# The x rows of a gated state-space block added by TensorE and copied out by ScalarE, and four products by C moved from GpSimd to VectorE

## The chip, the cores and the metric
One core of one Trainium2 chip runs the whole kernel. The metric is the device time of one execution in microseconds (us).

## The reference, cut to what matters
```
# ctx (4,512,256), x (4,512,512)
u  = silu(conv(ctx @ in_w.T) + b)                  # (4, 512 channels, 512 times)
dt, B, C from u @ xp_w.T ; dt = softplus(dt @ dt_w + bias)
state = state * exp(dt * A) + (dt * u) * B         # scan over time, 16 states per channel
y = sum over states(state * C) + D * u
y = y * silu(layernorm(x))                         # the gate
x = x + tanh(g_xattn) * y
x = x + tanh(g_ffn) * ffn(layernorm(x))            # w3(silu(w1 x) * (w2 x)), quantized
```

## The kernel before, in words
The state-space part is cut into 128 steps k. A step holds 128 channels (a block q), two of the 16 states and all 512 times, or, in the last two of the four batches (SPLIT), four states and half the times. Its tile hh (six buffers, NH = 6) is 128 x 1024. Eight steps make one group g = k // 8, whose y is summed in one PSUM bank, bank_y. The written-out order of each engine goes by a loop over slots k:

- GpSimd (POOL): product of step k by C, times_c, L808 and L813, then the product of step k+4 by B, times_b, L697 and L703. The latter waits until step k-2 has been summed out of its buffer (LEAD = 4, NH = 6). Small GpSimd operations (rh_pool, L1108) stand between them.
- VectorE (DVE): the scan of step k+3 (L765, L768), and for steps in BY_VECTOR also its product by C (times_c_vector, L791). Such a scan writes into the PSUM bank da that holds the exponentials, and the exponentials of step k+2, which use the same bank, wait for the product.
- ScalarE (ACT): the exponentials of step k+4 (exp, L731 and L738, into one of two PSUM banks da), which wait for the scan of step k+2, and keep_state (L751), which saves the last state of a first half.
- TensorE (PE): sums(k-1), eight transposes into bank_y (L846). At the first step of a group it waits for bank_y to be free and puts D*u into it first (L834, the seed).

The second part (the gated MLP, on tiles of 128 rows, TILE gives the slot of each) runs in the same loops: a_tensor and b_tensor (L1001, L1010), tanh_scalar (L1022), gated_vector (L1029, L1035), square_scalar (L1040), hq_scalar (L1104), transposes ht_tensor (L1155) and their copies hqt_scalar (L1166), out_tensor (L1186). At slots 49, 64, 87 and 99 dt_scalar (L337, L340) computes softplus, with a table load before it and one after it, for the next groups. z_scalar (L518, L519) and xt_tensor (L968) prepare gates and MLP inputs.

At slots 40, 48, ..., 120 the group g = k // 8 - 1 is finished. In gate, VectorE multiplies bank_y by the gate (L571) and adds the rows of x, writing x2 (L586, or L580 in the SPLIT batches). The mark ("y", g) of that add is what sums(k) of TensorE waits for. Groups 0 to 3 go another way (y_keep and y_first), and group 15 stands in the tail after the loops. In slots 38 to 79 sums(k-1) is TensorE's first work of a slot; the copy hqt_scalar(i, 1) is late in ScalarE's slot.

Of the kernel before, what the change touches and what calls it, by code (L numbers as in the profile page):

```python
# [12 lines left out]
P = 128  # L13
# [3 lines left out]
NE = DM // P  # L17
# [40 lines left out]

BY_VECTOR = (14, 16, 25, 45, 49, 53, 62, 67, 68, 73, 77)


def c_by_vector(k):
# [27 lines left out]
def build(nc, book, x, ctx_t, in_w, xp_w, dt_w, weights, consts, out):  # L92
    u_dram = nc.dram_tensor("u_scratch", [NB, P, NE, L], F32).ap()
    xd_dram = nc.dram_tensor("xd_scratch", [NB, ROWS, L], F32).ap()
    with ExitStack() as ctx:
# [114 lines left out]
        BV, BP = line("first_products"), line("first_rows_of_b")  # L210
        ZV, ZA, ZG, ZP = line("z_vector"), line("z_scalar"), line("z_pool"), line("z_tensor")
        WV, WA, WP = line("weight_vector"), line("weight_scalar"), line("weight_tensor")
        YV, YA = line("y_vector"), line("y_scalar")
        MV, MA, MP, MG = line("mlp_vector"), line("mlp_scalar"), line("mlp_tensor"), line("mlp_pool")

        hl = sb("hl", [P, NE, NS])
# [348 lines left out]
            YV.did(v.tensor_tensor(columns(x2[0], g), by_rows(bank_t[:, :]), columns(xin, g), ALU.add), ("p", g))  # L565

        def gate(v, g):
            b, q = g // NE, g % NE
            v.wait_ge(s_sum, STEPS * (g + 1))
            v.wait_ge(*ZA.of(("gT", g)))  # L570
            YV.did(v.tensor_tensor(bank_y[:, :], bank_y[:, :], gbuf[:, q, :], ALU.mult))  # L571
            if b in SPLIT:
                h, p = q // 2, q % 2
                if p == 0:
                    for t in (2 * h, 2 * h + 1):
                        v.wait_ge(*d_out[t].of(NE * (b - 2) + t))
                v.wait_ge(*YV.now())
                to, rows = [of[:, 2 * h:2 * h + 2, 2 * p * P:2 * (p + 1) * P].rearrange("p c (j d) -> p j c d", j=2)
                            for of in (x2[b % 2], xin)]
                YV.did(v.tensor_tensor(to, bank_y[:, :].rearrange("p (j c d) -> p j c d", j=2, c=2), rows, ALU.add),  # L580
                       ("y", g))
                return
            if g == NE:
                v.wait_ge(*WA.of(("sign", NW - 1)))
            v.wait_ge(*YV.now())
            YV.did(v.tensor_tensor(columns(x2[b % 2], q), by_rows(bank_y[:, :]), columns(xin, q), ALU.add), ("y", g))  # L586

        def x_done(i):

            b = i // NE  # L590
            if b == 0:
                return YV.of(("p", NE - 1))
            return YV.of(("y", NE * b + (1 if b in SPLIT and i % NE < 2 else NE - 1)))

# [222 lines left out]
        def sums(pe, k):  # L817
            b, q, s = where(k)
            g = k // STEPS
            if s == 0:  # L820
                if g > NE:
                    pe.wait_ge(*YV.of(("y", g - 1)))
                elif g:
                    pe.wait_ge(*YA.of(("y", g - 1)))
                else:
                    pe.wait_ge(*PV.of("diag_d"))
                    pe.wait_ge(*BV.of(1))
                if g < NE:
# [375 lines left out]
        with nc.Block() as block:  # L1204
# [214 lines left out]
            def _(act):  # L1419
# [62 lines left out]
                for k in range(38, 80):  # L1482
                    for i in range(END):
                        c = k - tile_slot(i) - 1
                        if 0 <= c < NCH:
                            tanh_scalar(act, i, c)
                    if k + LEAD - 2 < ALL:
                        keep_state(act, k + LEAD - 2)
                    for i in range(END - 1):
                        if k == tile_slot(i) + 9:  # L1490
                            hqt_scalar(act, i, 2)
                    if k + LEAD < ALL:
                        exp(act, k + LEAD)
                    for i in range(END - 1):
                        if k == tile_slot(i) + 8:
                            hqt_scalar(act, i, 0)
                    for first, n, done in TURNS:
                        if k == done + 3:
                            center_scalar(act, first, n)
                    for i in range(END + 1):  # L1500
                        if k == tile_slot(i) - 2:
                            xr_scalar(act, i)
                    for n in PAIR:
                        if k == PAIR[n]:
                            dt_scalar(act, 2 * n)
                            dt_scalar(act, 2 * n + 1)
                    for i in range(END):
                        if k == tile_slot(i) + 7:
                            hq_scalar(act, i, 0)
                            hq_scalar(act, i, 1)  # L1510
                    for i in range(END - 1):
                        if k == tile_slot(i) + 9:
                            hqt_scalar(act, i, 3)
                    for i in range(END):
                        if k == tile_slot(i) + 2 or k == tile_slot(i) + 4:
                            square_scalar(act, i, k - tile_slot(i) - 1)
                    for b in range(NB):
                        if k == (13, 34, 66, 94)[b]:
                            z_scales(act, b)
                    for i in range(END - 1):  # L1520
                        if k == tile_slot(i) + 8:
                            hqt_scalar(act, i, 1)
                    for i in TILES:
                        if i >= NE and k == z_turn_slot(i):
                            z_turn_scalar(act, i)
                    for i in TILES:
                        if k == z_slot(i):
                            z_scalar(act, i)
                    for i in range(END + 1):
                        if k == tile_slot(i) - 1:  # L1530
                            xqt_scalar(act, i)
                    for first, n, done in TURNS:
                        if k == done + 5:
                            rows_scalar(act, first, min(n, END - first))
                            if first + n > END:
                                rows_scalar(act, END, 1)
                for k in range(80, SLOTS):
                    for first, n, done in TURNS:
                        if k == done + 3:
                            center_scalar(act, first, n)  # L1540
                    for i in range(END):
                        c = k - tile_slot(i) - 1
                        if 0 <= c < NCH:
                            tanh_scalar(act, i, c)
                    if k + LEAD < ALL:
                        exp(act, k + LEAD)
                    if k + LEAD - 2 < ALL:
                        keep_state(act, k + LEAD - 2)
                    for i in range(END + 1):
                        if k == tile_slot(i) - 2:  # L1550
# [38 lines left out]
                    for i in range(END - 1):  # L1589
                        if k == tile_slot(i) + 8:  # L1590
                            hqt_scalar(act, i, 1)
                act.preload_act_table_set("silu_and_others")
                tanh_scalar(act, 13, 0)
                hq_scalar(act, 12, 0)
# [42 lines left out]
            def _(pe):  # L1637
# [39 lines left out]
                for k in range(38, 80):  # L1677
# [34 lines left out]
                    for i in range(END + 1):  # L1712
                        c = k - tile_slot(i)
                        if 0 <= c < NCH:
                            b_tensor(pe, i, c)
                for k in range(80, SLOTS):
                    if 0 <= k - 1 < ALL:
                        sums(pe, k - 1)
# [32 lines left out]
                    for i in range(END + 1):  # L1751
                        c = k - tile_slot(i)
                        if 0 <= c < NCH:
                            b_tensor(pe, i, c)
                sums(pe, 125)
                sums(pe, 124)
                ab_tensor(pe, 13, 1)
# [282 lines left out]
```

## Time and profile before

| | |
|---|---|
| Device time, median of 3 runs | 658.8 us (657.06, 658.80, 659.78) |
| Profiled execution, span from first to last instruction | 658.2 us (its own device time is not listed apart) |
| GpSimd (POOL) busy | 588.0 us, 89% |
| VectorE (DVE) busy | 585.5 us, 89% |
| ScalarE (ACT) busy | 535.6 us, 81% |
| TensorE (PE) busy | 503.0 us, 76% |
| Mean granted TensorE clock | 0.919 |

Busy times are sums over the whole span. Times in the rows below are counted from the start of the span. A time in square brackets behind an instruction is how long its engine stood idle before it, and which instruction ended that.

### The profile page before, as it was taken

What the parts mean: (1) busy time and instruction counts of PE and PEld (TensorE: products, weight loads), DVE (VectorE), ACT (ScalarE), POOL (GpSimd) and SP (SyncE); (2) the same over time, 40 slices, a digit from 0 to 9 for tenths busy, and PEclk for the clock granted to TensorE, in tenths of its full rate; (3) what the DMA queues carried; (4) which work ended last, traced back from release to release, by engine and by line L of the source; (5) the groups of instructions that cost most, each with busy time, mean ns of one, the idle gap of its engine ahead of it and who ended that gap; (6) DMA issues with size and microseconds to landing.
All of it is one profiled execution on the core that took longest, in us unless ns stands there. A gap on an engine that the chain in (4) does not pass through costs nothing.

```text
span 658.2 us, 7987 instructions
## 1 busy us (share of the span) xinstructions
PE 503.0 (76%) x2560; PEld 310.1 (47%) x2560; DVE 585.5 (89%) x771; ACT 535.6 (81%) x997; POOL 588.0 (89%) x289
## 2 busy tenths in 40 slices
PE   8798888993565777788658586877767786768997
PEld 3254534552453445555535354554444544446554
DVE  6779779998998899999889999999897999999765
ACT  6754757788999688978888798898899898897764
POOL 1399999998999999999999999999999999999331
PEclk9898989998766979999796999889899999899999
DMA  5698687579950100256500000046700000000001
GB/s 184 199 406 295 209 298 277 192 274 392 394 223 6 33 0 1 75 171 234 179 21 1 32 1 16 1 146 224 269 17 0 17 1 16 1 17 17 0 18 47
DMA packets 24473, 80.77 MB, mean 123 GB/s; under 512 B 2464, under 2 KB 5152, under 8 KB 21360
## 3 DMA queue, kind: packets, MB, share of 16 engines
q1 hardware_dynamic: 24432, 80.27, 33.7%
q8 instruction: 20, 0.33, 0.2%
q14 instruction: 21, 0.17, 0.1%
HBM read 72.53 MB, written 7.73 MB: 122 GB/s over the span
## 4 chain that ended last, share of the span: by engine, by line
POOL 31%; DVE 23%; PE 15%; ACT 15%; issue 10%; DMA 5%; SPq 2%; DVEq 0%; POOLq 0%; ACTq 0%
POOL hh L703 9%; DVE hh L768 9%; POOL hh L813 8%; POOL hh L808 7%; POOL hh L697 6%; ACT da L731 4%; DVE hh L765 3%; DMA wq<-x 3%; DVE room L1029 2%; PE da L1186 2%; PE bank_y L846 2%; PE bank_b L1010 2%; DVE sm L1074 2%; PE bank_a L1001 1%; ACT room L1166 1%
## 5 line engine op out<-in xcount | busy, mean ns | idle before, releaser
L768 DVE TENSOR_TENSOR_SCAN hh<-da,hh 128x1024 f32<-128x1024 f32 x85 | 193.4, 2280 | 3.4 <-ACT da L738 2.3
L846 PE MATMUL bank_y<-ident,hh 128*128 128x128 f32 x1024 | 144.5, 291 | 9.0 <-POOL hh L813 8.7
L846 PEld LDWEIGHTS bank_y<-ident,hh 128*128 128x128 f32 x1024 | 129.6, 152 | 37.4 <-issue 16.1
L808 POOL TENSOR_TENSOR hh<-hh,cc 128x1024 f32<-128x1024 f32 x60 | 141.7, 2364 | 1.7 <-ACT hl L751 1.5
L813 POOL TENSOR_TENSOR hh<-hh,cc 128x1024 f32<-128x1024 f32 x57 | 134.7, 2363 | 0.0
L703 POOL TENSOR_TENSOR hh<-pair,bb 128x1024 f32<-128x1024 f32 x30 | 70.7, 2358 | 26.3 <-DMA bb<-xd_scratch 23.9
L765 DVE TENSOR_TENSOR_SCAN hh<-da,hl,hh 128x256 f32<-128x256 f32 x128 | 85.4, 730 | 0.0
L703 POOL TENSOR_TENSOR hh<-wq,bb 128x1024 f32<-128x1024 f32 x32 | 75.5, 2367 | 2.4 <-PE bank_y L846 2.4
L697 POOL TENSOR_TENSOR hh<-wq,bb 128x1024 f32<-128x1024 f32 x32 | 75.8, 2370 | 0.8 <-PE bank_y L846 0.8
L697 POOL TENSOR_TENSOR hh<-pair,bb 128x1024 f32<-128x1024 f32 x32 | 75.2, 2352 | 1.2 <-PE bank_y L846 1.2
L738 ACT ACTIVATE da<-pair,cst 128x511 f32<-128x511 f32 x64 | 41.3, 679 | 23.5 <-DVE hh L768 23.5
L731 ACT ACTIVATE da<-wq,cst 128x256 f32<-128x256 f32 x128 | 53.3, 464 | 7.8 <-DVE hh L765 7.5
L731 ACT ACTIVATE da<-pair,cst 128x255 f32<-128x255 f32 x128 | 53.0, 461 | 1.7 <-DVE hh L768 1.7
L1001 PE MATMUL bank_a<-wq,room 128*128 128x512 fp8e4 x120 | 33.6, 405 | 26.5 <-DVE room L1029 23.9
L738 ACT ACTIVATE da<-wq,cst 128x511 f32<-128x511 f32 x64 | 41.4, 683 | 8.9 <-DVE hh L768 8.7
L1022 ACT ACTIVATE room<-bank_a,sm 128x512 f32<-128x512 f32 x58 | 39.2, 676 | 7.9 <-PE bank_a L1001 7.6
L1186 PE MATMUL bank_t<-wq,room 128*128 128x512 fp8e4 x192 | 43.4, 379 | 2.1 <-ACT room L1166 2.1
L1001 PE MATMUL bank_a<-wq,xqT 128*128 128x512 fp8e4 x112 | 32.4, 417 | 16.0 <-DVE room L1029 16.0
L1166 ACT ACTIVATE room<-bank_t,sm 128x512 bf16<-128x512 f32 x53 | 35.8, 676 | 10.8 <-PE bank_t L1155 10.7
L1029 DVE SCALAR_TENSOR_TENSOR room<-room,bank_a 128x512 f32<-128x512 f32 x52 | 35.3, 679 | 9.3 <-ACT room L1022 8.9
L1010 PE MATMUL bank_b<-wq,room 128*128 128x512 fp8e4 x120 | 33.4, 404 | 0.0
L968 PE MATMUL bank_t<-ident,room 128*128 128x128 f32 x56 | 10.2, 312 | 27.0 <-ACT room L951 15.2
(269 smaller groups left out, 1085.7 us busy)
## 6 DMA issues: line engine op xcount, KB each, us to landing
bb<-xd_scratch SPq DMA_DIRECT2D x32, 512.0 KB, 5.1
cc<-xd_scratch SPq DMA_DIRECT2D x32, 512.0 KB, 7.5
wq<-weights SPq DMA_DIRECT2D x12, 1024.0 KB, 6.7
stage<-weights SPq DMA_DIRECT2D x8, 1024.0 KB, 5.6
xin<-x SPq DMA_DIRECT2D x4, 1024.0 KB, 5.5
room<-weights SPq DMA_DIRECT2D x4, 1024.0 KB, 8.0
u_scratch<-wq SPq DMA_DIRECT2D x6, 512.0 KB, 3.0
wq<-x SPq DMA_DIRECT2D x2, 1024.0 KB, 18.2
```

Of the source, the lines that this page charges most:

```text
L697: ins = g_.tensor_tensor(quarters(flat(hh[k % NH])), du2[g % 4][:, HALF * (q % 2):HALF * (q % 2 + 1)].unsqueeze(1).to_broadcast([P, 4, HAL ...
L703: ins = g_.tensor_tensor(hh[k % NH][:, :, :], du2[g % 4].unsqueeze(1).to_broadcast([P, GN, L]), bb[:, s * GN:(s + 1) * GN, :], ALU.mult)
L731: ins = act.activation(da[:, j, first:HALF], dt2[g % 4][:, HALF * (q % 2) + first:HALF * (q % 2 + 1)], ACT.Exp, scale=a_neg[:, q, n + j:n ...
L738: ins = act.activation(dbank[k % 2][:, j, 1:L], dt2[g % 4][:, 1:L], ACT.Exp, scale=a_neg[:, q, s * GN + j:s * GN + j + 1])
L765: ins = v.tensor_tensor_scan(to[:, t], da[:, t], h[:, t], hl[:, q, n + j:n + j + 1], ALU.mult, ALU.add)
L768: ins = v.tensor_tensor_scan(to, da, h, 0.0, ALU.mult, ALU.add)
L808: ins = g_.tensor_tensor(quarters(flat(hh[k % NH])), quarters(flat(hh[k % NH])), cc[:, n:n + 4, t], ALU.mult)
L813: ins = g_.tensor_tensor(hh[k % NH][:, :, :], hh[k % NH][:, :, :], cc[:, s * GN:(s + 1) * GN, :], ALU.mult)
L846: mm = pe.matmul(bank_y[:, (first + c) * P:(first + c + 1) * P], flat(hh[k % NH])[:, at:at + P], ident[:, :], start=False, stop=(s == STEP ...
L1001: mm = pe.matmul(a[:, :], xqT[i % 2][:, k, :], w1q[:, k, c * 512:(c + 1) * 512], start=(k == 0), stop=(k == NE - 1))
L1029: MV.did(v.scalar_tensor_tensor(out=th[c % 2], in0=th[c % 2], scalar=1.0, in1=a[:, :], op0=ALU.add, op1=ALU.mult), ("g", i, c))
L1186: mm = pe.matmul(bank_g(i)[:, :], hqT[:, f, :], w3q[:, f, :], start=(f == 0), stop=(f == KF - 1))
```

## The change
The rows of x are no longer added by VectorE for groups 4 to 14. TensorE adds them in bank_y, by a float32 matmul with the identity, and ScalarE copies bank_y into x2. TensorE's step stands last in its slot k (k = 40, 48, ..., 120), and so does ScalarE's copy in its own slot; sums(k), at the head of TensorE's next slot, waits for the copy. Group 15 keeps both steps on VectorE. Steps 58, 65, 100 and 107 are added to BY_VECTOR, so their product by C goes from GpSimd to VectorE. From slot 80 on, keep_state of a step in BY_VECTOR goes ahead of the exponentials in ScalarE's slot. Readers of x2 wait for ScalarE's mark.

```diff
-BY_VECTOR = (14, 16, 25, 45, 49, 53, 62, 67, 68, 73, 77)
+BY_VECTOR = (14, 16, 25, 45, 49, 53, 58, 62, 65, 67, 68, 73, 77, 100, 107)
...
         def gate(v, g):
-            b, q = g // NE, g % NE
+            q = g % NE
             v.wait_ge(s_sum, STEPS * (g + 1))
             v.wait_ge(*ZA.of(("gT", g)))
-            YV.did(v.tensor_tensor(bank_y[:, :], bank_y[:, :], gbuf[:, q, :], ALU.mult))
...
+            YV.did(v.tensor_tensor(bank_y[:, :], bank_y[:, :], gbuf[:, q, :], ALU.mult), ("gated", g))
+            if g == NB * NE - 1:
...
+        def x_add_tensor(pe, g):
+            pe.wait_ge(*YV.of(("gated", g)))
+            if g % NE == 0:
+                pe.wait_ge(*d_x.of(g // NE))
+            if g // NE in SPLIT:
+                for j in range(2):
+                    mm = pe.matmul(bank_y[:, 2 * P * j:2 * P * (j + 1)], ident[:, :], y_place(xin, g)[:, j, :, :],
+                                   start=False, stop=(j == 1), skip_group_check=True)
+            else:
+                mm = pe.matmul(bank_y[:, :], ident[:, :], y_place(xin, g), start=False, stop=True,
+                               skip_group_check=True)
+            YP.did(mm, ("x", g))
+
+        def y_scalar(act, g):
+            b, q = g // NE, g % NE
+            act.wait_ge(*YP.of(("x", g)))
...
+            YA.did(act.activation(y_place(x2[b % 2], g), rows, ACT.Copy), ("y", g))
...
             if s == 0:
-                if g > NE:
-                    pe.wait_ge(*YV.of(("y", g - 1)))
-                elif g:
+                if g:
                     pe.wait_ge(*YA.of(("y", g - 1)))
...
+                    if k % STEPS == 0 and PER < k < ALL:
+                        y_scalar(act, k // STEPS - 1)
...
+                    if c_by_vector(k + LEAD - 2):
+                        keep_state(act, k + LEAD - 2)
                     if k + LEAD < ALL:
                         exp(act, k + LEAD)
-                    if k + LEAD - 2 < ALL:
+                    if k + LEAD - 2 < ALL and not c_by_vector(k + LEAD - 2):
                         keep_state(act, k + LEAD - 2)
...
+                    if k % STEPS == 0 and PER < k < ALL:
+                        x_add_tensor(pe, k // STEPS - 1)
```

## Rows read from the trace of the kernel before

**Rows 1.** The page: busy time, share and instructions of each engine.
```profile
PE 503.0 (76%) x2560; PEld 310.1 (47%) x2560; DVE 585.5 (89%) x771; ACT 535.6 (81%) x997; POOL 588.0 (89%) x289
```

**Rows 2.** Five of 837 pieces of the last-ending chain: start, length, what.
```profile
241.62 0.52 POOL sm L1108
...
325.66 1.28 ACT L337
...
482.99 1.16 ACT room L1040 x2
...
518.50 2.36 POOL hh L697
...
607.08 4.65 POOL hh L808 x2
```

**Rows 3.** Busy time in stretches: length; PE, PEld, DVE, ACT, POOL; clock, DMA share, GB/s.
```profile
264.00:319.00 55.00, 42.29 (x266) 27.99 (x264) 54.07 (x57) 45.80 (x80) 55.00 (x26) 1.00 0.47 162
...
518.00:612.00 94.00, 69.81 (x434) 45.89 (x433) 89.29 (x147) 80.05 (x166) 93.44 (x46) 0.98 0.03 12
```

**Rows 4.** Instruction groups by line and shape: busy us, mean ns, idle before.
```profile
L808 POOL TENSOR_TENSOR hh<-hh,cc 128x1024 f32<-128x1024 f32 x60 | 141.7, 2364 | 1.7 <-ACT hl L751 1.5
...
L791 DVE TENSOR_TENSOR hh<-da,cc 128x1024 f32<-128x1024 f32 x11 | 13.5, 1225 | 0.4
...
L545 ACT ACTIVATE gbuf<-bank_t,sm 128x512 f32<-128x512 f32 x12 | 8.0, 668 | 0.0
...
L251 PE MATMUL bank_a<-wq,room 128*128 128x512 f32 x16 | 7.7, 602 | 0.0
```

**Rows 5.** VectorE in order of time: a gate (slot 40) and a product by C.
```profile
222.36 0.69 DVE L571 TENSOR_TENSOR bank_y<-bank_y,gbuf 128x512 f32<-128x512 f32 x1
223.16 0.69 DVE L586 TENSOR_TENSOR stage<-bank_y,xin 128x512 f32<-128x512 f32 x1
223.77 2.28 DVE L768 TENSOR_TENSOR_SCAN hh<-da,hh 128x1024 f32<-128x1024 f32 x1
...
234.22 1.22 DVE L791 TENSOR_TENSOR hh<-da,cc 128x1024 f32<-128x1024 f32 x1
235.36 1.21 DVE L1074 TENSOR_REDUCE sm<-room 128x1 f32<-128x1024 f32 x1
```

**Rows 6.** Slots 48 and 49 in order of time.
```profile
260.13 0.76 ACT L519 ACTIVATE bank_a<-xin,sm 128x512 f32<-128x512 f32 x1
...
262.73 0.63 PE L968 MATMUL bank_t<-ident,room 128*128 128x128 f32 x4 [1.62 <-DVE room L1193]
...
264.42 0.60 ACT L337 ACTIVATE pair<-bank_a 128x512 f32<-128x512 f32 x1 [0.97 <-PE bank_a L300]
```

**Rows 7.** Slots 63 to 65 in order of time.
```profile
320.14 0.22 DVE L1093 TENSOR_SCALAR sm<-sm 128x1 f32<-128x1 f32 x1 [1.15 <-POOL sm L1108]
...
320.82 2.37 ACT L1104 ACTIVATE wq<-wq,sm 128x1024 f32<-128x1024 f32 x2
...
327.68 1.04 PE L846 MATMUL bank_y<-ident,hh 128*128 128x128 f32 x8
...
328.96 0.68 ACT L1166 ACTIVATE room<-bank_t,sm 128x512 bf16<-128x512 f32 x1
...
329.79 0.63 PE L1155 MATMUL bank_t<-ident,wq 128*128 128x128 f32 x4 [1.07 <-ACT room L1166]
...
334.27 2.29 DVE L768 TENSOR_TENSOR_SCAN hh<-da,hh 128x1024 f32<-128x1024 f32 x1 [1.04 <-ACT da L731]
```

**Rows 8.** ScalarE in slot 89, in order of time.
```profile
440.12 1.27 ACT L731 ACTIVATE da<-wq,cst 128x256 f32<-128x256 f32 x3 [0.20 <-DVE hh L765]
```

**Rows 9.** Slot 104 in order of time: ScalarE's last gate operation, TensorE's seed, GpSimd's wait.
```profile
519.07 0.55 ACT L519 ACTIVATE bank_a<-xin,sm 128x256 f32<-128x256 f32 x1
...
516.50 1.05 PE L834 MATMUL bank_y<-diag_d,pair 128*128 128x128 f32 x8
...
518.50 2.36 POOL L697 TENSOR_TENSOR hh<-pair,bb 128x1024 f32<-128x1024 f32 x1 [0.44 <-PE bank_y L846]
```

More of the change, by code:

```diff
@@ L212, in build @@
         WV, WA, WP = line("weight_vector"), line("weight_scalar"), line("weight_tensor")
-        YV, YA = line("y_vector"), line("y_scalar")
+        YV, YA, YP = line("y_vector"), line("y_scalar"), line("y_tensor")
         MV, MA, MP, MG = line("mlp_vector"), line("mlp_scalar"), line("mlp_tensor"), line("mlp_pool")
@@ L567, in gate, with y_place @@
         def gate(v, g):
-            b, q = g // NE, g % NE
+            q = g % NE
             v.wait_ge(s_sum, STEPS * (g + 1))
             v.wait_ge(*ZA.of(("gT", g)))
-            YV.did(v.tensor_tensor(bank_y[:, :], bank_y[:, :], gbuf[:, q, :], ALU.mult))
+            if g == NE:
+                v.wait_ge(*WA.of(("sign", NW - 1)))
+            YV.did(v.tensor_tensor(bank_y[:, :], bank_y[:, :], gbuf[:, q, :], ALU.mult), ("gated", g))
+            if g == NB * NE - 1:
+                for t in (2, 3):
+                    v.wait_ge(*d_out[t].of(NE + t))
+                v.wait_ge(*YV.now())
+                YV.did(v.tensor_tensor(y_place(x2[1], g), bank_y[:, :].rearrange("p (j c d) -> p j c d", j=2, c=2),
+                                       y_place(xin, g), ALU.add), ("y", g))
+        def y_place(of, g):
+            b, q = g // NE, g % NE
+            if b in SPLIT:
+                h, p = q // 2, q % 2
+                return of[:, 2 * h:2 * h + 2, 2 * p * P:2 * (p + 1) * P].rearrange("p c (j d) -> p j c d", j=2)
+            return columns(of, q)
+        def x_add_tensor(pe, g):
[11 more added lines that the diff above has]
+        def y_scalar(act, g):
+            b, q = g // NE, g % NE
+            act.wait_ge(*YP.of(("x", g)))
             if b in SPLIT:
@@ L575, in gate @@
                     for t in (2 * h, 2 * h + 1):
[L576 to L586, printed above, removed]
+                        act.wait_ge(*d_out[t].of(NE * (b - 2) + t))
+                rows = bank_y[:, :].rearrange("p (j c d) -> p j c d", j=2, c=2)
+            else:
+                rows = by_rows(bank_y[:, :])
+            YA.did(act.activation(y_place(x2[b % 2], g), rows, ACT.Copy), ("y", g))
         def x_done(i):
@@ L592, in x_done @@
                 return YV.of(("p", NE - 1))
-            return YV.of(("y", NE * b + (1 if b in SPLIT and i % NE < 2 else NE - 1)))
+            g = NE * b + (1 if b in SPLIT and i % NE < 2 else NE - 1)
+            return (YV if g == NB * NE - 1 else YA).of(("y", g))
         def sum_slot(i):
@@ L1591, in _ @@
                             hqt_scalar(act, i, 1)
+                    if k % STEPS == 0 and PER < k < ALL:
+                        y_scalar(act, k // STEPS - 1)
                 act.preload_act_table_set("silu_and_others")
@@ L1715, in _ @@
                             b_tensor(pe, i, c)
+                    if k % STEPS == 0 and PER < k < ALL:
+                        x_add_tensor(pe, k // STEPS - 1)
                 for k in range(80, SLOTS):
@@ L1754, in _ @@
                             b_tensor(pe, i, c)
+                    if k % STEPS == 0 and PER < k < ALL:
+                        x_add_tensor(pe, k // STEPS - 1)
                 sums(pe, 125)
```

## The prediction, made before the changed kernel was run
> **What bounds the kernel now.** I read the page's busy shares first, then the chain that ended last, then the busy time by stretches, and last the order of time around each slot that the change touches. The page says that no engine is the bound by itself: GpSimd and VectorE are both at 89% [rows 1]. The stretches sharpen that: from 264 to 319 us GpSimd is busy 55.00 of 55 us and VectorE 54.07; from 518 to 612 us they have 93.44 and 89.29 of 94 [rows 3]. So a busy share can't say which of the two a saved microsecond is saved on. The chain can. It goes along GpSimd up to its small operation at 241.62, then leaves it, and until 518.50 runs through VectorE, ScalarE and TensorE, among others through ScalarE's softplus stage at 325.66; from GpSimd's product at 518.50 it stays on GpSimd to the last products at 607.08 [rows 2]. What I take from it: between 242 and 518 us, GpSimd's work hides behind a VectorE and ScalarE path that is just as long; after 518 us VectorE's work hides behind GpSimd's. I therefore follow the change along this path and add up what each edit does to it. A plus is lateness.
>
> **The parts and their prices.**
>
> *Add of x taken off VectorE, 11 times.* At slot 40 the gate starts at 222.36, the add at 223.16 and the scan at 223.77 [rows 5]. Without the add the scan could start some 0.6 us behind the gate, as the scan does behind the add: 1.41 - 0.61 = 0.8 us saved on VectorE's path. Eleven times that is 8.8 us, but only where VectorE's path is the one that counts. At slot 40 GpSimd's is, so that one is worth nothing.
>
> *Product by C on VectorE, 4 times.* It takes 1225 ns against 2364 ns on GpSimd [rows 4]. The next instruction starts 1.14 us behind it, 0.1 before its end (235.36 against 234.22 + 1.22) [rows 5]. The product needs its scan's result and can't overlap that scan's end in this way, so I add 0.1 and the wait itself: 1.3 us more for VectorE in all. GpSimd is relieved of 2.4 us each time.
>
> *TensorE's matmul with the identity.* A float32 matmul 128 x 512 by two records of 602 ns, pipelined, is between 0.6 and 1.2 us [rows 4]; I take 0.9. It is hidden where TensorE would wait for ScalarE's copy anyway, which is so at slots 48, 64 and 104 (below).
>
> *ScalarE's copy.* By the 128 x 512 copies out of PSUM, 668 ns, some 0.6 from start to start [rows 4]; 11 of them, 7 us more on ScalarE.
>
> *The new wait.* This is what decides. sums(k), at the head of TensorE's slot k+1, used to wait for VectorE's add. Now it waits for a copy that is the last thing in ScalarE's slot k. Behind sums(k) on TensorE stand the transposes and MLP matmuls of slot k+1, and behind sums(k) by its buffer stands GpSimd's product by B of step k+6. On ScalarE the next tanh and exponentials stand behind the copy. Slot by slot:
>
> - Slot 48: ScalarE ends its z work at 260.13 + 0.75 = 260.9 [rows 6]. Copy to 261.5, seed and sums about 0.9 us each [rows 7, 9] to 263.3; the transpose L968 behind them starts then instead of at 262.73, where it had waited 1.62 us for VectorE. The softplus stage waits for TensorE (0.97 us before L337) [rows 6], so the path gets +0.6, and VectorE's saving of this slot is lost.
> - Slot 56: VectorE's path counts: -0.8. Its product of step 58 stands just ahead: +1.3.
> - Step 65: VectorE has 1.15 us idle in which the product would nearly fit, but the exponentials of step 67 wait for it, and behind these ScalarE is solid (L1104 at 320.82 for 2.37, then the exponentials of step 68) [rows 7]: +1.3 on ScalarE's path. Sum so far +2.4.
> - Slot 64: the softplus stage. Before, sums(64) was done at 328.7, and the transpose L1155 waited for ScalarE's L1166 (328.96 to 329.64) until 329.79 [rows 7]. ScalarE's copy comes only behind that L1166: 329.6 to 330.2; then seed and sums 1.8 us, then L1155 at 332.1. That is 2.3 us later, and ScalarE's next copy, the table load and exponentials behind it, and the scan at 334.27, which waited 1.04 us for them [rows 7], all follow. +2.3. Sum +4.7.
> - Slots 72 and 80: -0.8 and -0.7; ScalarE has room there. Sum +3.2.
> - Slot 88: ScalarE had 0.20 us idle before the exponentials at 440.12 [rows 8]. A copy of 0.67 ahead of them makes it 0.5 late, and the hq and tanh behind them hand that to VectorE: +0.5 instead of -0.8. Sum +3.7.
> - Slot 96: tanh one copy later, so -0.3 only; then the product of step 100 ahead of the work that ScalarE's 482.99 waits for [rows 2]: +1.3. Sum +4.7.
> - Slot 104: ScalarE ends z at 519.62 [rows 9], 0.8 earlier with the add gone. Copy to 519.45, seed to 520.5, sums to 521.4, where it was 516.50 + 0.9 + 1.04 = 518.4 [rows 9]: +3.0. GpSimd's product at 518.50 already waited 0.44 us for these sums. Sum +7.7.
> - From there GpSimd sets the end, without the product of step 107: -2.4 [rows 4]. Slots 112 and 120 shorten only VectorE, which by then has 4.7 - 3 x 0.8 + 1.3 = +3.6 and hides again. Sum +5.3.
>
> 0.6 - 0.8 + 1.3 + 1.3 + 2.3 - 0.8 - 0.7 + 0.5 - 0.3 + 1.3 + 3.0 - 2.4 = +5.3 us. The products of 58, 65 and 100 give nothing: they relieve GpSimd of 7.1 us where it is off the path, and what it gains it waits for at sums(104). xin is loaded later too, by the SP queue, which waits for ScalarE's mark; some 6 us later at slot 65 (the mark goes from some 324 to 330 us), hidden since the first z work on it is in slot 68, three slots of two GpSimd products each, some 14 us, later [rows 4].
>
> The profiled execution spans 658.2 us; the median of the runs is 658.8, 0.6 above it, so the same sum on the median is **664.1 us**.
>
> **Bounds of what the trace doesn't show.** The matmul of x with its two ends (0.6, 1.2) is off the path in the three slots that cost most; at 1.2 it adds 0.3 at up to three others, +1. A copy is 0.57 to 0.7. The three stalls (0.6, 2.3, 3.0) come from queue orders; each is bounded below by nothing (work before it absorbs it) and above by adding ScalarE's own lateness again, some 0.7. So the likeliest case has its own range of +2.5 to +9, 661.3 to 668.
>
> **A rule against this.** The Trainium skill (Perfetto Trace Analysis, Identifying the Most-Contended Engine) says to take the engine with the highest occupancy as the one to optimize first, and that occupancy is a fair measure for VectorE, ScalarE and GpSimd. By this rule the sum would be the first rival's.
>
> **The rivals.**
>
> 1. *GpSimd alone bounds.* Four products less, 4 x 2.364 = 9.5 us [rows 4], come off the end: 649.3. For it: 55.00 of 55 us [rows 3]. Against it: the chain leaves GpSimd for 276 us [rows 2], and VectorE stands at 54.07 of 55. Chance 0.10. This ends on the other side, and decides if VectorE and ScalarE can move up by as much as GpSimd.
> 2. *VectorE alone bounds and the new waits cost nothing.* -11 x 0.8 + 4 x 1.3 = -3.6 us: 655.2. For it: it is the engine most on the chain from 264 to 319, idle 0.93 of 55 us. Against it: the 0.20 us and the 1.07 us above show that ScalarE and TensorE have no room in slots 64 and 88. It decides if the copy is done by the time the add used to be. Chance 0.12.
> 3. *One of the two large stalls is absorbed* (2.3 at slot 64 or 3.0 at slot 104), for instance because sums(104) is late but GpSimd has caught up before: +2.3 to +3, 661.1 to 661.8, no change that can be told. Chance 0.22.
> 4. *The copy costs more*: ScalarE waits for TensorE at the end of every slot and hands it on each time, 0.7 us at six more slots: +9.5, 668.3. For it: ScalarE is 80.05 of 94 us busy at the end [rows 3], but with gaps of a microsecond before most exponentials, so I hold it unlikely. Chance 0.11.
>
> My forecast has 0.45. A measurement of this kernel tells about 0.5% from no change, here 3.3 us. Faster by more (under 655.5): all of rival 1 and most of 2, 0.20. Within: the rest of 2, rival 3, 0.24. Slower by more (over 662.1): forecast and rival 4, 0.56. The range goes from rival 2 to rival 4, 655 to 669, and leaves out rival 1 and the edges.
>
> **What the changed profile would show.** If right: the chain still leaves GpSimd before slot 48 and passes, near 330 us, through the ScalarE copy into x2, then L834, L846 and L1155; L1155 stands 2 us and more behind L1166; the scan of step 69 has an idle time of some 4 us instead of 1.04, ended by ScalarE; GpSimd's product of step 110 waits some 3 us or more for bank_y. GpSimd is busy near 579 us, VectorE near 583, ScalarE near 543. Rival 1 or 2 is right if the copies stand well ahead of the seeds, and these start as soon behind the gates as before. The weakest points are slot 104, since a late sums(104) counts only as far as nothing else has held GpSimd up, and the claim that GpSimd's relief before slot 104 is worth nothing.

## The result and the profile after

The changed kernel takes **666.2 us** (median of 6 runs, 665.3 to 667.7) where the kernel before, on the same chip in the same minutes, takes 659.1 (6 runs, 657.1 to 662.0). The ratio is **1.0108, 95% interval [1.0087, 1.0129]**: 7.1 us slower, between 5.7 and 8.5. The forecast was 664.1, slower, with 655 to 669 as the range. The profiled execution spans 663.6 us, 5.4 more than that of before; the medians lie 7.1 apart, so the profiled executions show some 1.7 us less of a difference than the medians do. Single runs of the kernel before lie up to 2.8 us from its median, and I compare places within one pair of traces to some tenths only where the start of the stretch agrees. The trace of the changed kernel runs 0.3 us ahead of that of before up to slot 40, so a place that is said to be 5.2 us later has lost 5.5.

The page's first part, against [rows 1]:
```profile
PE 514.8 (78%) x2596; PEld 317.1 (48%) x2596; DVE 582.8 (88%) x764; ACT 541.9 (82%) x1012; POOL 579.3 (87%) x285
```
GpSimd has 8.7 us less work and VectorE 2.7 less; ScalarE has 6.3 more and TensorE 11.8 more. Forecast were 579, 583 and 543 for the first three. Both engines that seemed full became lighter and the kernel became slower, so what was taken away was waited for. The waits of GpSimd say at which hand-over, first of before, then of after (engine, line and what it waited for: us in total, times, longest):
```profile
POOL hh L697 <- PE bank_y L846: 2.1, 3, 0.8
```
```profile
POOL hh L726 <- PE bank_y L873: 13.8, 5, 5.9
```
GpSimd's product by B (L697, now L726) waits for the sums (L846, now L873) 11.7 us more than before. That is more than the 8.7 us it was relieved of. The copy's own line shows who waits for it, over the whole span (us, times):
```profile
L614 ACT ACTIVATE stage<-bank_y x7: 574/597/607, 224.3 to 597.4; 128x512 f32<-128x512 f32 x7
L614 ACT ACTIVATE room<-bank_y x4: 577/588/597, 366.5 to 478.4; 128x512 f32<-128x512 f32 x4
...
who waited for it (us, times):
...
  PE bank_y L861: 11.5, 11
```
The seed (L861, once L834) stands behind ScalarE's copy all 11 times, and TensorE is idle 11.5 us there.

Two stretches of the windows, against [rows 3], and between them the one that lost most (length; PE, PEld, DVE, ACT, POOL; clock, DMA share, GB/s):
```profile
264.00:319.00 55.00, 43.60 (x272) 28.81 (x271) 52.99 (x57) 46.39 (x82) 54.09 (x26) 1.00 0.48 155
319.00:346.00 27.00, 18.34 (x91) 12.75 (x90) 20.24 (x25) 22.19 (x53) 17.09 (x9) 0.75 0.22 79
...
518.00:612.00 94.00, 74.54 (x439) 48.30 (x438) 88.76 (x140) 82.99 (x176) 91.45 (x44) 0.95 0.03 12
```
From 319 to 346 us, around slot 64, GpSimd is busy 17.09 of 27 us, where it had been 26.20 before. None of the other stretches read has such a hole. In it GpSimd waits 9.9 us for the sums. Not all of that is loss: in e3 below, where the stall of slot 64 is undone, it still waits 5.9 us there, and in e9, where only the products of steps 58 and 65 have left it, 6.3 us: relieved of these it is ahead, and waits.

**Slot 64**, against [rows 7], in order of time, ScalarE first, then TensorE, VectorE and GpSimd:
```profile
326.88 0.67 ACT L1193 ACTIVATE room<-bank_t,sm 128x512 bf16<-128x512 f32 x1
...
330.87 0.68 ACT L1193 ACTIVATE room<-bank_t,sm 128x512 bf16<-128x512 f32 x1
331.43 0.61 ACT L614 ACTIVATE stage<-bank_y 128x512 f32<-128x512 f32 x1
...
329.39 1.02 PE L598 MATMUL bank_y<-xin,ident 128*128 128x512 f32 x2
332.09 1.16 PE L861 MATMUL bank_y<-diag_d,pair 128*128 128x128 f32 x8 [1.68 <-ACT stage L614]
333.09 1.04 PE L873 MATMUL bank_y<-ident,hh 128*128 128x128 f32 x8
333.96 0.60 PE L1182 MATMUL bank_t<-ident,wq 128*128 128x128 f32 x4
...
338.42 2.29 DVE L797 TENSOR_TENSOR_SCAN hh<-da,hh 128x1024 f32<-128x1024 f32 x1 [3.28 <-ACT da L760]
...
334.21 2.36 POOL L726 TENSOR_TENSOR hh<-pair,bb 128x1024 f32<-128x1024 f32 x1 [3.58 <-PE bank_y L873]
```
The reader is to see the queue: the copy L614 is the last of ScalarE's slot, behind the softplus stage and L1193; the matmul of x (L598) had been done a microsecond earlier and TensorE waits 1.68 us for the copy. The transpose L1182, which stood at 329.79 before, starts at 333.96, and the scan of step 69 at 338.42 instead of 334.27. Part of these 4.2 us was carried in: the copy starts at 331.43, 1.8 us later than the 329.6 that the prediction worked out without the lateness summed up to there.

**Slot 104**, against [rows 9]:
```profile
522.91 0.55 ACT L519 ACTIVATE bank_a<-xin,sm 128x256 f32<-128x256 f32 x1
523.40 0.57 ACT L614 ACTIVATE stage<-bank_y 128x512 f32<-128x512 f32 x1
...
521.17 1.03 PE L595 MATMUL bank_y<-xin,ident 128*128 128x256 f32 x4
524.03 1.16 PE L861 MATMUL bank_y<-diag_d,pair 128*128 128x128 f32 x8 [1.83 <-ACT stage L614]
525.02 1.04 PE L873 MATMUL bank_y<-ident,hh 128*128 128x128 f32 x8
...
526.14 2.36 POOL L726 TENSOR_TENSOR hh<-pair,bb 128x1024 f32<-128x1024 f32 x1 [2.55 <-PE bank_y L873]
```
The seed, 516.50 before, stands at 524.03. GpSimd's product stands at 526.14 instead of 518.50: +7.6 us, where the sum had +7.7.

**The chain that ended last** (start, length, what) at slot 64, and at the end, where it had been GpSimd's in [rows 2]:
```profile
330.95 0.60 ACT room L1193
331.55 0.50 ACT stage L614
...
332.09 1.16 PE bank_y L861 x8
333.25 0.89 PE bank_y L873 x8
...
334.21 2.36 POOL hh L726
```
```profile
524.49 1.14 DVE hh L820
525.65 0.18 ACT hl L780
...
526.10 1.59 ACT da L760 x4
...
597.40 0.61 ACT stage L614
...
609.12 2.58 DVE hh L794 x4
```
The first piece is the one forecast. The second is not: from slot 104 to 612 us the chain of after runs through VectorE, ScalarE and TensorE, not along GpSimd, and it enters this stretch through the product of step 107 on VectorE (L820). Later it passes through ScalarE's copy once more (L614 at 597.40, slot 120), a place where the forecast had no wait.

### The profile page after: what moved, and what is told of

Same layout as the page of the kernel before. It is cut to its first block, busy times and chain, and to the rows that moved or that the text cites. A ratio compares the mean times of both kernels' runs of the same rounds, so it can differ in the third digit from the quotient of the medians.

```text
span 663.6 us, 8066 instructions
## 1 busy us (share of the span) xinstructions
PE 514.8 (78%) x2596; PEld 317.1 (48%) x2596; DVE 582.8 (88%) x764; ACT 541.9 (82%) x1012; POOL 579.3 (87%) x285
## 4 chain that ended last, share of the span: by engine, by line
POOL 28%; DVE 22%; ACT 19%; PE 15%; issue 10%; DMA 5%; SPq 2%; POOLq 0%; DVEq 0%; ACTq 0%
POOL hh L732 9%; POOL hh L842 8%; POOL hh L726 6%; DVE hh L797 5%; DVE hh L794 5%; ACT da L760 5%; POOL hh L837 4%; DMA wq<-x 3%; DVE da L797 2%; DVE room L1056 2%; PE da L1213 2%; PE bank_b L1037 2%; PE bank_a L1028 2%; PE bank_y L873 2%; DVE sm L1101 2%
## 5 line engine op out<-in xcount | busy, mean ns | idle before, releaser
L797 DVE TENSOR_TENSOR_SCAN hh<-da,hh 128x1024 f32<-128x1024 f32 x81 | 184.2, 2279 | 5.4 <-ACT da L760 3.3
L873 PE MATMUL bank_y<-ident,hh 128*128 128x128 f32 x1024 | 145.8, 292 | 9.7 <-POOL hh L842 8.2
L873 PEld LDWEIGHTS bank_y<-ident,hh 128*128 128x128 f32 x1024 | 130.2, 152 | 39.9 <-issue 16.4
L837 POOL TENSOR_TENSOR hh<-hh,cc 128x1024 f32<-128x1024 f32 x57 | 135.1, 2370 | 2.3 <-ACT hl L780 2.2
L842 POOL TENSOR_TENSOR hh<-hh,cc 128x1024 f32<-128x1024 f32 x56 | 132.4, 2365 | 0.0
L726 POOL TENSOR_TENSOR hh<-pair,bb 128x1024 f32<-128x1024 f32 x32 | 75.5, 2366 | 13.8 <-PE bank_y L873 13.8
L726 POOL TENSOR_TENSOR hh<-wq,bb 128x1024 f32<-128x1024 f32 x32 | 76.0, 2375 | 0.0
L760 ACT ACTIVATE da<-wq,cst 128x256 f32<-128x256 f32 x128 | 53.3, 466 | 3.9 <-DVE hh L794 3.7
L760 ACT ACTIVATE da<-pair,cst 128x255 f32<-128x255 f32 x128 | 53.0, 461 | 0.8 <-DVE hh L797 0.7
L1028 PE MATMUL bank_a<-wq,room 128*128 128x512 fp8e4 x120 | 33.5, 405 | 19.8 <-DVE room L1056 17.6
L1213 PE MATMUL bank_t<-wq,room 128*128 128x512 fp8e4 x192 | 45.1, 390 | 2.0 <-ACT room L1193 2.0
L1193 ACT ACTIVATE room<-bank_t,sm 128x512 bf16<-128x512 f32 x53 | 35.9, 677 | 12.1 <-PE bank_t L1182 12.0
L1028 PE MATMUL bank_a<-wq,xqT 128*128 128x512 fp8e4 x112 | 30.7, 399 | 10.9 <-DVE room L1056 10.9
L797 DVE TENSOR_TENSOR_SCAN da<-da,hh 128x1024 f32<-128x1024 f32 x15 | 34.3, 2288 | 0.0
L1037 PE MATMUL bank_b<-wq,room 128*128 128x512 fp8e4 x120 | 33.5, 404 | 0.0
```

What stands on the lines that cost most here:

```text
L726: ins = g_.tensor_tensor(quarters(flat(hh[k % NH])), du2[g % 4][:, HALF * (q % 2):HALF * (q % 2 + 1)].unsqueeze(1).to_broadcast([P, 4, HAL ...
L760: ins = act.activation(da[:, j, first:HALF], dt2[g % 4][:, HALF * (q % 2) + first:HALF * (q % 2 + 1)], ACT.Exp, scale=a_neg[:, q, n + j:n ...
L797: ins = v.tensor_tensor_scan(to, da, h, 0.0, ALU.mult, ALU.add)
L837: ins = g_.tensor_tensor(quarters(flat(hh[k % NH])), quarters(flat(hh[k % NH])), cc[:, n:n + 4, t], ALU.mult)
L842: ins = g_.tensor_tensor(hh[k % NH][:, :, :], hh[k % NH][:, :, :], cc[:, s * GN:(s + 1) * GN, :], ALU.mult)
L1028: mm = pe.matmul(a[:, :], xqT[i % 2][:, k, :], w1q[:, k, c * 512:(c + 1) * 512], start=(k == 0), stop=(k == NE - 1))
```

## The experiments

Twelve kernels. Each ratio is to the kernel before on the same chip; us are the ratio less 1, times 659. An interval is some 1.1 to 2 us wide to either side, so two of these kernels are told apart only when they differ by some 2 us.

| kernel | ratio, 95% interval | us |
|---|---|---|
| e1 the four products only | 1.0094 [1.0068, 1.0121] | +6.2 |
| e2 the eleven adds only | 1.0109 [1.0085, 1.0133] | +7.2 |
| e3 changed, slot 64's add back | 1.0059 [1.0037, 1.0080] | +3.9 |
| e6 product 107 only | 1.0041 [1.0022, 1.0061] | +2.7 |
| e4 changed, copies of 64 and 104 early | 1.0066 [1.0048, 1.0085] | +4.3 |
| e5 changed, slot 104's add back | 1.0109 [1.0086, 1.0131] | +7.2 |
| e7 adds of 56, 72, 80, 112, 120 only | 1.0002 [0.9986, 1.0017] | +0.1 |
| e10 before, four products left out | 1.0004 [0.9986, 1.0022] | +0.3 |
| e9 products 58 and 65 only | 1.0038 [1.0017, 1.0060] | +2.5 |
| e11 four products, 100 and 107 near their scans | 1.0080 [1.0051, 1.0108] | +5.3 |
| e12 before, eleven adds left out | 0.9974 [0.9953, 0.9995] | -1.7 |
| e13 before, both left out | 0.9906 [0.9876, 0.9936] | -6.2 |

**One part alone: e1, e2, e6.**
```
e1   gate() and its users as before;  BY_VECTOR = (..., 58, ..., 65, ..., 100, 107)
e2   gate() changed;                  BY_VECTOR = (14, 16, 25, 45, 49, 53, 62, 67, 68, 73, 77)
e6   gate() as before;                BY_VECTOR = (14, ..., 77, 107)
```
e1 and e6 keep the state ahead of the exponentials, as the changed kernel does; no step from 80 on is in e2's BY_VECTOR, so nothing changes there.

> Only the four products by C (steps 58, 65, 100, 107) go to VectorE; all adds of x stay on VectorE as before. Path theory: +1.3 us for each of steps 58, 65 and 100 on the VectorE and ScalarE path up to GpSimd's product of step 110, which gives GpSimd's end 3.9 - 2.4 = +1.5; VectorE's own end, which was only 0.2 us ahead of GpSimd's, gets four times 1.3 = +5.2. So the kernel is slower by some 5 us (4 to 6), ratio 1.006 to 1.009, with the scans late behind the steps 58, 65, 100, 107. GpSimd-bound rival: faster by up to 9.5 us, ratio 0.986.

> Only the eleven adds of x move to TensorE and ScalarE; the products by C stay as before. Path theory: nothing up to slot 64 (what VectorE saves is taken by its wait for GpSimd's L1108 in slot 63, and 0.6 is lost at slot 48), +2.3 at slot 64, -1.5 at slots 72 and 80, about 0 at slots 88 and 96, +3.0 at slot 104, GpSimd solid from there: +3 to +4.5 us, ratio 1.005 to 1.007. Rival (the adds are a gain for VectorE, the busiest on the path): -3 to -8 us, ratio below 0.996.

> The kernel before with the product of step 107 alone on VectorE. In this stretch (after GpSimd's product of step 110) GpSimd is on the chain and without an idle time, so the GpSimd-bound view expects -2.4 us, ratio 0.9964. Path theory: VectorE's end was only 0.2 us ahead of GpSimd's and gets +1.3, so +1 us, ratio 1.0015, no gain from relieving the engine that the chain names.

Each part alone costs nearly as much as the whole, and e6 costs 2.7 us where the prediction's term for it was -2.4. All three cost more than was expected of them (4 to 6, 3 to 4.5 and 1 us). The trace of e6 shows the reason on VectorE, then on ScalarE (here L829 is the product by C, L806 the scan, L789 the state's copy, L769 the exponentials):
```profile
517.51 1.21 DVE L829 TENSOR_TENSOR hh<-da,cc 128x1024 f32<-128x1024 f32 x1
518.64 2.28 DVE L806 TENSOR_TENSOR_SCAN hh<-da,hh 128x1024 f32<-128x1024 f32 x1
```
```profile
518.76 0.17 ACT L789 ACTIVATE hl<-da 128x4 f32<-128x4 f32 x1 [2.20 <-DVE hh L829]
...
519.14 1.65 ACT L769 ACTIVATE da<-pair,cst 128x255 f32<-128x255 f32 x4
```
From slot 80 on the product stands last in VectorE's slot, behind a reduction, the output's operation and z. ScalarE, which must keep the state and refill the buffer that the product reads, is idle 2.20 us. GpSimd is relieved of 2.4 us, but VectorE's scans are 2.3 us later by step 111 than they were at step 107, more than the product's own 1.3. And GpSimd has to wait for that path: it is idle 2.16 us before its product by C at 523.23, until ScalarE, behind these exponentials, has kept a state (L789), and 0.81 us more before the next product by B.

In e2's trace TensorE's clock fell in slot 96 (TensorE, ScalarE, VectorE):
```profile
474.20 1.91 PE L1037 MATMUL bank_b<-wq,room 128*128 128x512 fp8e4 x4
...
475.91 1.82 PE L595 MATMUL bank_y<-xin,ident 128*128 128x256 f32 x4
...
477.76 0.60 ACT L614 ACTIVATE room<-bank_y 128x512 f32<-128x512 f32 x1 [2.19 <-PE bank_y L595]
...
478.97 0.69 DVE L1056 SCALAR_TENSOR_TENSOR room<-room,bank_a 128x512 f32<-128x512 f32 x1 [2.94 <-ACT room L1049]
```
The granted clock from 474 to 478 us was 0.57, and the matmul of x took 1.82 us instead of the 1.03 of slot 104 above. ScalarE's queue passed that on: tanh stands behind the copy, and VectorE waited 2.94 us. The scan of step 100 comes 1.7 us later for it than in e3, e4 and e5, which had the full clock there. This can't be taken off e2's +7.2, which is the median of six runs within 1.4 us of each other, and the profiled executions of before and of the changed kernel had such a fall themselves, a slot earlier (last section). The expectation of +3 to +4.5 was too low, and I can't say by which wait.

**One stall undone: e3, e5.**
```
MOVED = all groups 4 to 14 but 7 (e3) or 12 (e5); for g not in MOVED, in gate():
    v.wait_ge(*YV.now())
    YV.did(v.tensor_tensor(y_place(x2[b % 2], g), rows, y_place(xin, g), ALU.add), ("y", g))
```


> The changed kernel, but the add of group 7 (slot 64, in the softplus stage) stays on VectorE; ten adds move. Path theory: the stall of 2.3 us at slot 64 is gone, the rest stays: 2.0 to 2.5 us faster than the changed kernel, so 4.5 us slower than before, ratio 1.0070 against 1.0108. Scan of step 69 late by some 2 us instead of 4.4. Rival: if lateness at slot 64 is absorbed later, no difference from the changed kernel.

> The changed kernel with the add of x of slot 104 alone back on VectorE. The prediction's own reading, in which sums(104) sets GpSimd's end: 3.0 us faster than the changed kernel, ratio 1.006. The reading from the changed kernel's trace, in which VectorE's and ScalarE's path is by then just as late (5.4 us at step 125, with exp(109) 6.5 us late behind the product of step 107): GpSimd's product by B of step 110 comes 3 us earlier, the end does not move, or by the add's 0.8 us to the late side: ratio 1.009 to 1.012.

The add of slot 64 back on VectorE gives back 7.1 - 3.9 = 3.2 us. The add of slot 104 back gives nothing (1.0109 against 1.0108), though GpSimd's product there no longer waits. GpSimd in e5 (L846 the product by C, L735 that by B):
```profile
518.27 2.38 POOL L846 TENSOR_TENSOR hh<-hh,cc 128x1024 f32<-128x1024 f32 x1
520.60 2.36 POOL L735 TENSOR_TENSOR hh<-pair,bb 128x1024 f32<-128x1024 f32 x1
```
No idle time, where the changed kernel has 2.55 us. But GpSimd comes to a wait two products later, behind ScalarE's keep_state and so behind the product of step 107:
```profile
527.99 2.36 POOL L846 TENSOR_TENSOR hh<-hh,cc 128x1024 f32<-128x1024 f32 x1 [2.16 <-ACT hl L789]
```
With 0.94 us more at the product by B after it, these are the 3 us again. The stall was real and worth nothing: the path through VectorE and ScalarE is by then as late, and GpSimd waits for it. A gain of 3.0 us would have shown; one of less than some 2 us would not.

**The queue order alone: e4.**
```
slot 64:  PE   + x_add_tensor ahead of dt_proj          ACT  + y_scalar right behind exp
slot 104: PE   + x_add_tensor behind out_tensor(0, 1)   ACT  + y_scalar behind xr, ahead of the z work
          both: - the same call at the end of the slot
```


> The changed kernel, but in slots 64 and 104 the matmul of x and ScalarE's copy stand early in their queues (slot 64: the matmul ahead of the dt projection, the copy right behind the exponentials; slot 104: the matmul behind the first output block, the copy ahead of the z work). Against the changed kernel. My theory of queue orders: the two stalls at sums(64) and sums(104) shrink by 1.7 and 2 us; product by B of step 110 on GpSimd is no longer 3.5 us late against its neighbours. VectorE's end, which was as late as GpSimd's in the changed kernel, gives back only what slot 64 gave: 1.7 to 3.7 us faster than the changed kernel, ratio to the kernel before 1.007 (1.005 to 1.009). Rival, the stalls only take the place of others (absorbed): no faster than the changed kernel, ratio 1.011. Rival, the stalls were all there is to the loss: 4 to 5 us faster than the changed kernel, ratio 1.003.

Same instructions, two places: 7.1 - 4.3 = 2.8 us less, ratio 1.0066 for the 1.007 expected. ScalarE's copies and GpSimd's product in e4:
```profile
326.87 0.60 ACT L623 ACTIVATE stage<-bank_y 128x512 f32<-128x512 f32 x1
...
517.24 0.60 ACT L623 ACTIVATE stage<-bank_y 128x512 f32<-128x512 f32 x1 [0.67 <-PE bank_y L604]
```
```profile
520.77 2.35 POOL L735 TENSOR_TENSOR hh<-pair,bb 128x1024 f32<-128x1024 f32 x1 [0.45 <-PE bank_y L882]
```
The copy of slot 64 stands at 326.87 instead of 331.43, and GpSimd's wait in slot 104 is back at 0.45, against 0.44 in [rows 9]. By e5 the second of these places is worth nothing, and GpSimd waits for keep_state here too (1.64 us). That leaves slot 64 for the gain. Between the scans of steps 67 and 69 the changed kernel falls back by 4.2 us against before, e4 by 2.6 and e3 by 1.2, so e4 undoes about half of the stall there. No kernel with one of the two places alone was run, and 2.8 us is known to some 2 us.

**Only the adds where no stall was expected: e7.**
```
BY_VECTOR as before;  MOVED = (6, 8, 9, 13, 14)
```


> The kernel before, with the add of x moved to TensorE and ScalarE only at slots 56, 72, 80, 112 and 120, where no queue stood behind the copy; products by C as before. Theory of the path: 0.8 us less at each of slots 56, 72 and 80 until GpSimd's path takes over, some 1 to 1.5 us less before slot 104, nothing behind it: 0.5 to 2 us faster than before, ratio 0.998 (0.996 to 1.000). Rival, each copy costs more than it gives wherever it stands: 1 to 4 us slower, ratio 1.003 to 1.006. Rival, VectorE alone bounds: 5 x 0.8 = 4 us faster, ratio 0.994.

1.0002: it costs nothing, and gives nothing that can be told. Its interval takes in -0.9 us, the better half of what I expected (0.996 to 0.998) is excluded. One reason is in its trace: in slot 120 TensorE waits 0.69 us for the copy, and the scan of step 125 comes 0.9 us later for it, so that place was not free. None of the versions tried that compute everything beats the kernel before.

**Which path bounds: e10, e12, e13.** These leave work out: in e10 four products by C aren't computed (step 69 stands in for 65), in e12 the rows of x are missing from eleven groups, in e13 both.
```
e10  BY_VECTOR = before's;  times_c(g_, k): if k in (58, 69, 100, 107): return
e12  gate(): x2 = bank_y * gbuf, and no add, for groups 4 to 14
e13  both
```


> The kernel before, with the products by C of steps 58, 69, 100 and 107 left out altogether (so the sums of these steps read what stands in the buffer): GpSimd is relieved of 4 x 2.36 us and nothing is added anywhere. Adds of x as before. Path theory: GpSimd's relief before slot 104 is worth nothing, the product of step 107 at most until VectorE's path takes over: 0.5 to 2 us faster than before, ratio 0.998 (0.996 to 1.000). Rival, GpSimd alone bounds: 9.5 us faster, ratio 0.986. In between, if VectorE's path moves up once GpSimd no longer holds its buffers: 3 to 5 us, ratio 0.993 to 0.995.

> The kernel before, with the adds of x of slots 40 to 120 left out (11 of them; the gate writes its product straight to x2, so these rows of the output lack x); products by C as before. VectorE is relieved of 11 x 0.8 us, GpSimd of nothing. Two paths of equal length: GpSimd's takes over after the first one or two adds saved: 0 to 2 us faster, ratio 0.999 (0.997 to 1.000). Rival, VectorE alone bounds: 8 us faster, ratio 0.988.

> Both at once: the 11 adds of x left out and the products by C of steps 58, 69, 100 and 107 left out, so that VectorE is relieved of 8.8 us and GpSimd of 9.5 us, with nothing put anywhere else. If before is bound by two paths of equal length, one through VectorE and ScalarE and one through GpSimd, the relief of both counts although that of GpSimd alone gave nothing (1.0004): 5 to 8 us faster, ratio 0.990 (0.988 to 0.993). Rival, a third path (ScalarE and TensorE) is just as long: 0 to 2 us faster, ratio 0.999.

The first parts of their pages, e10, then e12, then e13:
```profile
PE 497.8 (76%) x2560; PEld 305.9 (47%) x2560; DVE 585.0 (89%) x771; ACT 535.2 (82%) x997; POOL 579.5 (88%) x285
```
```profile
PE 502.9 (77%) x2560; PEld 311.3 (48%) x2560; DVE 578.3 (88%) x760; ACT 535.3 (82%) x997; POOL 587.9 (90%) x289
```
```profile
PE 497.3 (76%) x2560; PEld 307.0 (47%) x2560; DVE 577.8 (89%) x760; ACT 534.7 (82%) x997; POOL 578.9 (89%) x285
```
8.5 us of work off GpSimd, with nothing added anywhere, give +0.3 us: nothing that can be told. What GpSimd no longer computes it waits for: 6.8 us at its product by B for the sums, against 2.1 before. 7.2 us off VectorE give 1.7. Both together give 6.2, over four times what the two give apart (1.4). This is two paths of nearly equal length, and neither relief alone shortens the kernel by more than 1.7 us.

**Where the products cost: e9, e11.**
```
e9   BY_VECTOR = before's + (58, 65)
e11  e1, and in the slots from 80 on times_c_vector directly behind scan
```


> The kernel before, with only the products by C of steps 58 and 65 on VectorE; adds of x as before. The prediction's terms: 1.3 + 1.3 = +2.6 us on the path of VectorE and ScalarE, ratio 1.004. What the trace of both lets me expect now: +1.3 at step 58, +1.2 at step 69, half a microsecond given back by step 99, and GpSimd's end behind step 104 no later than that path has become: +1 to +2.6 us, ratio 1.0015 to 1.004. Rival, GpSimd bounds: 4.7 us faster, ratio 0.993.

> The kernel with the four products by C on VectorE and no add moved (1.0094 when the products of steps 100 and 107 stand at the end of VectorE's slot), now with these two right behind their scans. Theory of the queue order: exp(109) on ScalarE, which waits for the product of step 107 to free its buffer, starts 1 to 2 us earlier, and the end follows by about as much: ratio 1.007 (1.005 to 1.008). Rival, each product costs its own 1.2 us wherever it stands: no change against the other order, ratio 1.0094.

e9 is +2.5 us for the prediction's 1.3 + 1.3. With e6's +2.7, that leaves 6.2 - 2.5 - 2.7 = 1.0 us for the product of step 100 (forecast 1.3), known no better than to some 2 us; in e1's trace the scans are 1.3 us later behind it (steps 100 to 101). e11 is inconclusive: 0.9 us better than e1, with intervals that overlap widely. Its trace shows the wait moved as intended, on ScalarE:
```profile
520.64 0.17 ACT L789 ACTIVATE hl<-da 128x4 f32<-128x4 f32 x1
```
Nothing precedes it where e6 had 2.20 us; but the exponentials of the step after, which then wait for a scan that stands later, have 1.33 us idle before them in the same trace. The order moves more than half of the loss to a neighbour.

## Why the prediction was right, and where its terms were off

The sum was +5.3 us with a likeliest range of +2.5 to +9; measured is +7.1. The spans of the profiled executions differ by 5.4. The direction and the size came true; one of the mechanisms behind the sum did not, and that it did no harm to the total was luck.

**What bounds.** "GpSimd's relief before slot 104 is worth nothing" was called one of the two weakest points. e10 shows it, for the whole kernel: +0.3 us for four products less, one of them (step 69) not among the four that the change moves. The rule cited against the change (the Trainium skill, Perfetto Trace Analysis, Identifying the Most-Contended Engine: take the engine of highest occupancy first) would have had 9.5 us off the end. The trace and e10 disagree with it here, 89% and 89% being two paths and not one bound. Rival 1 is thereby out. Rival 2 is out by e12: eleven adds left out altogether, with no copy in their place, give 1.7 us and not 8.8.

**Slot 48, +0.6.** The softplus stage L337 starts at 264.52 for 264.42 before; since the after trace runs 0.3 us ahead up to slot 40 (the gate there starts that much earlier), that is +0.4.

**Products 58 and 65, +2.6.** e9: +2.5.

**Slot 64, +2.3.** This stall is the largest of the causes measured alone. Undoing it (e3) gives 3.2 us: the 2.3 of the stall, and 0.9 more that lies within the uncertainty of the two ratios (some 1.4 us each). In the changed kernel's trace the step from L1193 (1.9 us late) to the scan of step 69 (4.1 us late) is 2.2. Where the forecast placed a wait of "some 4 us" before the scan of step 69, the trace has 3.28. The reason given, a copy behind the softplus stage and L1166 at the end of ScalarE's slot, is borne out by e4, in which only places in the queues differ.

**Slot 88, +0.5.** Too high. The exponentials L760 that waited 0.20 us in [rows 8] had 3.1 us of lateness by then (the scans of steps 83 to 88 all start 3.1 us later than before), and the scan of step 93 starts 3.3 later: +0.2.

**Slot 104, +3.0; sum +7.7 on GpSimd.** GpSimd's product is 7.6 us late (526.14 - 518.50). The size is right, and what it was taken to mean is wrong: e5.

**"From there GpSimd sets the end, without the product of step 107: -2.4", and VectorE at +3.6 "hides again".** This is the step that failed. GpSimd's last products do come as forecast: they are 5.2 us later than before. But VectorE's last scans are 5.5 us late, not 3.6, and the chain runs through them. The forecast let VectorE's lateness fall by 1.1 us behind slot 104 (-0.8, +1.3, -0.8, -0.8); it rose by 1.3, from 4.2 at the scan of step 106 to 5.5. Term by term the trace has -0.4 at slot 104, +1.5 for the product of step 107, -0.7 at slot 112 and +0.9 at slot 120.

The largest of these errors is slot 120, which was to "shorten only VectorE". It is a fourth stall of the kind of slots 48, 64 and 104. The seed waits for the copy:
```profile
598.05 1.16 PE L861 MATMUL bank_y<-diag_d,wq 128*128 128x128 f32 x8 [0.69 <-ACT stage L614]
```
The transposes L1182, ScalarE's copy of them and tanh stand behind it, and VectorE is idle 0.75 us before the two operations ahead of the scan of step 125. The traces of e2, e3, e4, e5 and e7, which have this copy and the full clock at that place, show the same +0.9 at that scan; that of e10, without the copy and at the full clock, shows none. No kernel was run in which this copy alone is moved, so its price in the median isn't known.

The second error is the product of step 107. It stands last in VectorE's slot, and ScalarE waits for it (2.20 us in e6, 1.68 in the changed kernel) with the exponentials of step 109 behind it. The prediction counted such an exponentials' wait for step 65, and for step 107 only the product's own 1.3. It also took GpSimd's -2.4 as a gain of the whole, and e5 and e6 show GpSimd waiting for that other path instead. Measured alone, product 107 is +2.7 [+1.5, +4.0] and not -2.4, a term off by 5. In the changed kernel part of it was covered, since GpSimd's stall at slot 104 ran beside it: the scans lose 1.5 us there, 2.3 in e6. That the total was near is luck: GpSimd's path came out as forecast, and VectorE's, which was underrated by 1.9 us, only just overtook it.

**Parts don't add.** e1 and e2 add up to 13.4 us, both together are 7.1. In e2's trace GpSimd's last products are the later ones (5.9 us against 4.5 for VectorE's last scans), in e1's the two are nearly level (6.8 and 7.0); either way the end takes the later path, and what is lost on the other is hidden.

**The spans' 5.4 and the medians' 7.1.** Most of the 1.7 us between them is the choice of executions. In the runs of before that list both, the device time is 1.8 to 1.9 us above the span, so by estimate the profiled execution of before took 660.0, 0.9 above the median. That of the changed kernel took 665.8, 0.4 below its median, and its device time is 2.2 above its span.

**What stays open.** e2's +7.2 against 3 to 4.5 expected has no cause shown. The medians of e7 show that five of the copies, with the adds they replace, cost nothing together. How often TensorE's clock falls at a given place, and so how much of a median it makes, can't be read from one trace for each kernel.

## What to carry to other kernels

Where two engines stand at nearly 90% and the chain that ended last changes between them, ask of each edit which of the two paths it lengthens, and cut both or none: 8.5 us less on one gave nothing, the same with 7.2 less on the other gave 6.2. An operation handed to an engine with room costs by its place in that engine's queue and by who stands behind it, not by its 0.6 us: moved ahead in two of eleven slots, the same copies gave back 2.8 us. When two lateness sums run side by side to the end, carry both to the end with equal care, since the one that "hides" needs only a microsecond or two to be the bound.

## What the runs showed of the hardware

The clock granted to TensorE moved single executions by some 1.6 us at one place, in a kernel in which TensorE is busy 76% of the time. Around slot 96 the profiled execution of before had a granted clock of 0.55 to 0.60 (466 to 470 us), near the 1.2 GHz level, and its chain goes through the slow matmuls there:
```profile
466.26 1.89 PE bank_a L1001 x4
```
In e10, which differs from before only in four products, the same matmuls took 1.04 us at the full clock, and the scan of step 99 comes 1.6 us sooner behind that of step 98. The changed kernel had its fall at the same place (1.89 us at 469.30). So the two cancel in the comparison of their traces, and do not in one with e3 to e5, e6 or e10.

A fall on the chain need not cost anything. At 585.07 in the changed kernel four matmuls 128 x 512 (L1028) took 1.86 us, with a granted clock of 0.50 from 584 to 588 us, that is the 1.2 GHz level; TensorE had been idle 2.11 us before them:
```profile
585.07 1.86 PE L1028 MATMUL bank_a<-wq,room 128*128 128x512 fp8e4 x4 [2.11 <-ACT room L1000]
586.73 1.91 PE L1037 MATMUL bank_b<-wq,room 128*128 128x512 fp8e4 x4
...
590.79 1.03 PE L1037 MATMUL bank_b<-wq,room 128*128 128x512 fp8e4 x4
```
The same L1037 took 1.03 us four microseconds later. Against before, the scan of step 122 is 4.6 us late and that of step 124, behind these matmuls, is 4.6 us late too. In e3, at the full clock there, the two scans keep their distance just the same.

Idle time alone doesn't tell when the clock falls: TensorE of the kernel before was idle 2.53 us ahead of the same matmuls at 580.50 and ran them in 1.02, and 2.20 us ahead of those at 466.26, which took 1.89. The identity matmul of x, forecast at 0.9 us, took 1.02 to 1.03 at the full clock and 1.82 in slot 96 of e2.
